# Norms inside the remaining stages, loads in order of use, own banks for a second group, bias parts made once by GpSimd

## What is computed

```python
def _layernorm(x, axis=-1, eps=1e-05):
    m = jnp.mean(x, axis=axis, keepdims=True)
    v = jnp.var(x, axis=axis, keepdims=True)
    return (x - m) / jnp.sqrt(v + eps)
...
x = x + block(_layernorm(x, axis=-1), weights of the block)      # 16 times
```

## Time and profile before

| what | value |
|---|---|
| time, median of 3 runs | 3943.17 us (3942.64 to 3943.90) |
| the profiled execution | 3946.0 us, its span 3944.2 us |
| PE busy | 3227.8 us (82%), 21852 matmuls |
| DVE busy | 2328.7 us (59%) |
| ACT busy | 1703.2 us (43%) |
| POOL busy | 1110.0 us (28%) |
| DMA, mean | 42 GB/s over the span |
| chain that ended last | it ends in the last stage, no line has over 1% of the span |

### The profile page before, as it was taken

The page is one execution under the profiler, slowest core; times in us unless marked ns, Lnnn a source line. Parts: engine busy times, 40 slices in busy tenths (PEclk is TensorE's granted clock), DMA queues, the critical chain, the costliest instruction groups (busy, mean ns, idle before and its releaser), DMA issues. The chain is left out here.

```text
span 3944.2 us, 61118 instructions
## 1 busy us (share of the span) xinstructions
PE 3227.8 (82%) x21852; PEld 1684.0 (43%) x21852; DVE 2328.7 (59%) x5913; ACT 1703.2 (43%) x3496; POOL 1110.0 (28%) x601
## 2 busy tenths in 40 slices
PE   5898899896777777989688895788789786787778
PEld 2444444444666666434233341233234333353336
DVE  4666535445666666465289403898851349945992
ACT  2444433413222222243476425776643445633562
POOL 0000000001111111000289204999940006730771
PEclk8999999895555555999899997999999898998999
DMA  3332221120000000022100000000000101140114
GB/s 131 96 90 80 72 98 53 49 72 34 0 0 0 0 0 0 10 79 70 62 1 0 0 0 0 0 1 1 0 0 0 78 1 43 75 181 1 64 75 171
DMA packets 75647, 166.60 MB, mean 42 GB/s; under 512 B 9440, under 2 KB 46304, under 8 KB 66912
## 3 DMA queue, kind: packets, MB, share of 16 engines
q1 hardware_dynamic: 75488, 164.64, 12.3%
HBM read 120.57 MB, written 44.04 MB: 42 GB/s over the span
## 5 line engine op out<-in xcount | busy, mean ns | idle before, releaser
L1171 PE MATMUL psum<-h_ring,h_parts 128*128 128x4 bf16 (+2 forms) x12288 | 438.1, 170 | 164.4 <-ACT h_ring L1225 157.5
L2007 DVE TENSOR_TENSOR_SCAN s_hh<-psum,s_dbu 128x512 f32<-128x512 f32 x384 | 445.4, 1204 | 154.8 <-POOL s_dbu L1916 100.7
L1171 PEld LDWEIGHTS psum<-h_ring,h_parts 128*128 128x128 bf16 x12288 | 381.6, 105 | 223.3 <-ACT h_ring L1225 193.6
L1916 POOL TENSOR_TENSOR s_dbu<-s_du,s_bb 128x1024 f32<-128x1024 f32 x192 | 448.6, 2353 | 56.8 <-ACT s_bb L1859 53.3
L1225 ACT ACTIVATE h_ring<-h_pre 128x16 f32<-128x16 f32 x1024 | 174.9, 212 | 489.9 <-DVE h_pre L1282 484.3
L1746 PE MATMUL psum<-s_term,w_c 128*128 128x512 f32 x768 | 381.0, 612 | 0.0
L1874 ACT ACTIVATE psum<-s_delta,s_decay 128x512 f32<-128x512 f32 x384 | 263.3, 690 | 147.4 <-DVE s_hh L2007 140.5
L1282 DVE TENSOR_REDUCE h_pre<-psum 128x16 f32<-128x48 f32 x1024 | 170.4, 203 | 133.8 <-PE psum L1171 123.8
L851 DVE TENSOR_TENSOR f_hid<-f_gate,psum 128x512 f32<-128x512 f32 x184 | 126.1, 686 | 202.2 <-PE psum L777 194.6
L838 ACT ACTIVATE f_gate<-psum 128x512 f32<-128x512 f32 x184 | 109.7, 597 | 285.3 <-PE psum L773 285.3
L1524 PE MATMUL psum<-d_h,w_l2f 128*128 128x512 f32 x512 | 221.0, 592 | 0.0
(11 more groups left out here) (432 smaller groups left out, 6447.4 us busy)
## 6 DMA issues: line engine op xcount, KB each, us to landing
...
```

Source lines behind the costliest of these rows:

```text
L1171: mm = nc.tensor.matmul(columns_of(s // BLOCK, grp)[:, s % BLOCK, 0:3 - part, cols], parts[:, part, GROUP * grp + p, :], upper[:, (s - 1) ...
L1916: nc.gpsimd.tensor_tensor(dbu[:, s % 4], du[:, t % 2], both(bb[:, s % 4, :]), ALU.mult).then_inc(dbu_ready, 1)
L2007: nc.vector.tensor_tensor_scan(hh[:, s % 4, half, :], DECAYS[i % 3], dbu[:, s % 4, half, :], 0.0, ALU.mult, ALU.add).then_inc(scan_done, 1)
```

## The change

1. `layernorm` is removed; all 16 stages use `InnerNorm`. It gets `first` and `last` chunks, pieces that can be called one by one, and optionally a semaphore for each chunk's arrival. Each stage gives it banks and scratch tiles of its own.
2. The opening loads in the order of use: the columns of `c32` that the norm needs, chunk 0 of x, the first part of `l0a`, its rest, chunks 1 to 3, the small part of `cbf`, the rest of `c32`, `l2a`, `l3a`. SP waits for the first only. GpSimd casts the small table, now 512 columns. `pick_b` and `pick_c` become a tensor of their own, which the first scan loads into two tiles that are free at its start and GpSimd casts.
3. Latent attention: the norm of chunk 0, the QKV projection, and the other chunks' norm between the steps of turn 0. Turn 1 uses banks 0 and 1 (`low`, `high`). The scores of turn 0 use four banks. The output bias is added before the maxima of turn 0, not behind them. The loop's first two steps wait for `v_kept` and `q1_kept` of turn 1.
4. Recurrent heads: tanh of the weights first, the norms interleaved, the squares of the second one on DVE.
5. Unit attention: chunk 0 is normed before the first projections, chunks 1 to 3 between the second and the third. GpSimd makes the three bf16 parts of phi_b once, into `bias_parts`, for both soft expert stages, which drop their own.

```diff
-def layernorm(g):
...
+    def tensor(self, pe, first=0, last=CHUNKS):
+        for c in range(first, last):
+            if c == first:
+                self.centre_chunk(pe, c)
+            if c + 1 < last:
+                self.centre_chunk(pe, c + 1)
+            self.mean_chunk(pe, c)
...
@@ latent attention, PE @@
+                norm.tensor(pe, 0, 1)
+                pe.wait_ge(g.loaded["l0a_first"], 16)
+                pe.wait_ge(norm.normed, 1)
+                project_qkv(0, 0)
+                norm.centre_chunk(pe, 1)
+                norm.centre_chunk(pe, 2)
                 pe.wait_ge(g.loaded["l0a"], 16)
+                latents(0, 0)
+                norm.mean_chunk(pe, 1)
+                norm.centre_chunk(pe, 3)
+                latents(1, 0)
+                norm.mean_chunk(pe, 2)
+                norm.mean_chunk(pe, 3)
+                queries(0)
+                value_latents(0)
+                latents(0, 1)
+                values(0)
+                latents(1, 1)
...
@@ latent attention, DVE @@
+                norm.vector(dve, 0)
                 dve.wait_ge(g.loaded["l0a"], 16)
+                rope(0, 0)
+                norm.vector(dve, 1)
+                rope(1, 0)
+                norm.vector(dve, 2)
+                left(0, 0)
+                norm.vector(dve, 3)
+                third(0, 0)
...
@@ recurrent heads, ACT @@
                 act.wait_ge(g.loaded["l1a"], 16)
                 nc.scalar.activation(at[:, :], w["a"], ACT.Tanh).then_inc(weights_bounded, 1)
+                norm.scalar(act, 0, 3)
+                invert(0)
+                norm.scalar(act, 3, 4)
+                for j in range(1, CHUNKS):
+                    invert(j)
+                nc.scalar.preload_act_table_set("exp_and_others")
...
@@ selective scan, PE, GpSimd, SP @@
+                norm.tensor(pe)
                 pe.wait_ge(g.loaded[pack], 16)
+                pe.wait_ge(norm.normed, 1)
...
+                pe.wait_ge(norm.normed, CHUNKS)
+                pe.wait_ge(tables_cast, 2)
                 for s in range(3):
                     pick_b(s)
...
+                if tables:
+                    for table, there, loaded in picks:
+                        pool.wait_ge(loaded, 16)
+                        nc.gpsimd.tensor_copy(table.rearrange("p n m -> p (n m)"), wide(there)).then_inc(tables_cast, 1)
...
+                        sp.dma_start(wide(there), g.pick_tables[k]).then_inc(loaded, 16)
...
@@ unit attention, PE (in project) and GpSimd @@
+                    elif m == 2:
+                        norm.tensor(pe, 1, CHUNKS)
+                        pe.wait_ge(norm.logged, CHUNKS)
...
+                pool.wait_ge(g.loaded["l3f"], 16)
+                whole, part = g.w["l3f"]["phi_b"], g.bias_parts
+                nc.gpsimd.tensor_copy(part[:, :], whole).then_inc(hi_kept, 1)
+                pool.wait_ge(hi_kept, 1)
+                nc.gpsimd.tensor_tensor(left[:, :], whole, part[:, :], ALU.subtract).then_inc(rest, 1)
...
@@ soft experts, PE and DVE @@
+                    inner.tensor(pe)
                     for q in range(CHUNKS):
+                        pe.wait_ge(inner.normed, q + 1)
...
-                    pe.wait_ge(bias_set, PARTS)
...
-                    for c in range(PARTS):
-                        at = slice(c * CHUNK, (c + 1) * CHUNK)
-                        nc.vector.tensor_copy(bias[:, at], w["phi_b"][:, at]).then_inc(hi_kept, 1)
...
+                    for c in range(CHUNKS):
+                        inner.vector(dve, c)
...
@@ opening @@
+                    sp.dma_start(tensors["c32"][:, 0:few], args["c32"][:, 0:few]).then_inc(norms_loaded, 16)
+                    sp.dma_start(fixed(g.resid, 0), fixed(args["x"], 0)).then_inc(g.x_loaded[0], 16)
+                    sp.dma_start(tensors["l0a"][:, 0:some], args["l0a"][:, 0:some]).then_inc(g.loaded["l0a_first"], 16)
+                    sp.dma_start(tensors["l0a"][:, some:], args["l0a"][:, some:]).then_inc(g.loaded["l0a"], 16)
+                    for c in range(1, CHUNKS):
+                        sp.dma_start(fixed(g.resid, c), fixed(args["x"], c)).then_inc(g.x_loaded[c], 16)
+                    sp.dma_start(g.wide, args["cbf"]).then_inc(g.table_loaded, 16)
+                    sp.dma_start(tensors["c32"][:, few:], args["c32"][:, few:]).then_inc(g.loaded["c32"], 16)
...
+                    sp.wait_ge(norms_loaded, 16)
```

351 lines of the change are left out of this document (195 added, 156 removed).

## The result

The changed kernel takes 3882.8 us (median of 4 runs, 3876.1 to 3884.9); the kernel before, run beside it, takes 3943.5 us (3942.6 to 3946.9). The ratio is 0.9842, with a 95% interval of 0.9824 to 0.9859: 60.7 us less, where 55.8 were forecast (3887.4). In the profiled executions the span fell from 3944.2 to 3881.3 us, 62.9 less.

The account below looks back on a forecast made before the run. Sixteen stages run one after another on one core, so shorter ways from entry to long loop count: 18.8 + 6.7 + 3.6 + 4.6 + 0 + 10.0 + 12.1 = 55.8 off 3943.2 gives 3887.4 us, range 3873 to 3905.

Parts of the forecast that it names:

- The opening and the latent attention: From span start to the latent attention's loop: reordered loads, interleaved norm and more banks start it at 64.2, not 83.0: -18.8 us.
- PE at 6.2: Opening: PE's first matmul starts at 6.2 us, 11.7 us earlier, after SP's 11 issues and the barrier.
- the term of 0.45 us an issue: Opening: SP's 11 transfers are issued 0.45 us apart, so the last is out at 5.6 us.
- The recurrent heads: Entry to loop: ACT waits 3.4 us for weights, but cuts lie under the norm and the second norm follows chunk by chunk: -6.7 us.
- The scans: Two selective scans, entry to first convolution: the norm inside makes it 13.6 and 11.0 us, a gain of 3.6 and 4.6.
- If the clock holds: Scans' first convolutions: with PE idling only about 3.3 us, staying warm would gain 1.9 and 2.3 us more; left out of the forecast.
- The unit attention: Entry to sums of squares: little gain in the first stretch, sums perhaps at the low clock; taken as 0, bounds -3 and +4.
- little to gain: Unit attention's first stretch: with ACT's norms ahead of its exponentials, DVE's last lift ends 25.6 us after entry against 26.5.
- The soft expert stages: Entry to first logits in both stages: without DVE's bias parts they start at about 14.6 and 17.0 us: -10.0 and -12.1.
- (b): Rival: the norm inside is no shorter than outside where ACT is the chain; 3918.7 us, chance 0.09 with half-way cases.
- (c): Rival: slower, through one more low-clock stretch per scan turn and soft expert tile, 103 us in all; 3991 us, chance 0.02.
- (a): Rival: more overlap, with warm convolutions (-4.2), less waiting in the opening (-4), warm soft-stage transposes (-4); 3875 us, chance 0.10.

Follow-up runs that it names:

- the kernel with everything together: Changed kernel plus late opening issues, scan fillers, unit attention's norm ahead with fillers, two squares before tanh, two turning banks in soft stages: 3866.8 us, ratio 0.9800.

## Why the prediction was right, and where it was not

**The sum.** The time came out 4.6 us from the forecast, but the ways did not come out that near. The seven ways to the loops were forecast at 55.8 us and measured at 66.2, and all seven were too small, by 0.2 to 3.6 us each. What brought the total back was not in the sum: the loops behind the ways took 4.2 us in all (the unit attention alone 5.0), and the medians differ by 2.2 us less than the two profiled executions. The mechanism, a shorter way to each loop, is borne out in all seven stages; that the total is so close is in part luck.

**The opening and the latent attention, -18.8 forecast, -22.4 measured.** PE at 6.2 was wrong (7.91): the term of 0.45 us an issue holds for the first four, but three chunk issues took 0.86 each and the last four 0.5 to 0.6. First chunk normed: 13.2 said, 14.8 measured; end of the first group's last cut 35.1 and 36.3; second pair of the second group 37.1 and 38.1. First scores 49.1 and 48.1: I followed PE's chain, and the row names the stacked query parts, but only 0.33 us behind PE's own work; in the runs with all of x first, with the norm whole and with the late issues PE's own work is last. From the scores to the loop I counted 15.1 us (its terms add up to 14.8) and it took 12.5: the added bias (1.67) lies in front of the maxima as said, but these take 6.45 instead of 7.8. Four banks for two bring 3.3 us (9.8 against 6.45, in the kernel before and in the run with shared banks alike), and I had 2.0. That is the term mis-sized. Another 0.8 is the clock: the turning of the maxima took 1.04 us, and 1.87 in the kernel before, from which I had the 5.3 behind the last maximum. The stall of a_qr went as said in the changed kernel (in four of the variants the addition falls beside the last cast again and takes 0.87 to 1.82 us). It is not shown what the 4.4 us between PE's first matmul and the last cut are made of, beyond that stall (1.1): no run puts the separate norm back there.

**The recurrent heads, -6.7 and -8.2.** The added wait was at its place (tanh 3.5 us after the entry, 3.4 said), the last scaling ended 24.1 after it (24.2 said, from 915.6 - 891.4). Behind that it took 2.0 us instead of 3.4 to the loop: GpSimd's first laying, ahead of PE, 1.0 instead of 2.2, and the projection 1.0 instead of 1.2. That is the difference. The cuts were long done: before, two of them, with both inputs in SBUF, lay beside GpSimd's laying, whose first two steps took 0.69 and 1.37 us where each takes 0.41 now.

**The scans, -3.6 and -4.6 against -4.8 and -4.8.** My norm of 12.4 us at the low clock was too long for the first one: four centre passes took 3.16 instead of 3.75, and the last product ended 11.4 after the entry. "If the clock holds" came true in neither scan of the changed kernel, and in the first scan of four other runs.

**The unit attention, 0 and +3.3.** It is inside my bounds of -3 and +4, but not by my sum. The way to the sums is 1.7 us shorter, and the eight cold passes cost that 1.7 again (I allowed 2.9). The 3.3 are PE at the low clock behind them, 1.6 in each of the first two turns, which I had put at nothing. The scaling beside GpSimd was missed by 0.7 us where I gave it 0 to 1; where the variants hit it, it cost the rest of one GpSimd instruction, as I had taken from the rule. On the first stretch, "little to gain" because ACT has the norms ahead of its exponentials was wrong as a reason: the run with the norm ahead shows 7.8 us of gain there. ACT had been idle 6.4 us for PE's second centre pass, which I had not put in ACT's chain, since I took PE's small groups for the cost of the clock only.

**The soft expert stages, -10.0 and -12.1 against -11.1 and -13.2 (whole stages -10.4 and -16.4).** A round of transposes, copy and hand-over took 1.4 us instead of the 1.8 that I counted, because the transposes ran at the high clock (0.63 instead of 1.11 us); three rounds make the 1.1. The norm outside again and the bias on DVE show that both parts count: the norm is worth 4.5 and 6.6 us on the way to the logits, the bias 9.4 and 8.7 (together more than the 11.1 and 13.2 that both gave, since each hides a part of the other). The extra 3.2 us in the second stage's loop I had not foreseen: from its first logits on, the granted clock of the next 40 us was 0.87, against 0.82 before and 0.82 with the norm outside again, and from the first logits to the end it took 310.9 us, against 314.2 and 315.0. But the kernel with everything together has 0.87 too and 312.8 us, and in the first soft stage 0.80 stands beside 305.2 us and 0.83, with the bias on DVE, beside 308.7. The clock of these 40 us does not by itself give the length, and the cause stays open.

**The rivals.** (b) fell by the run with the norm outside. (c) asked for 27 or more low stretches; what came were a few, in the unit attention. (a), more overlap than counted, was right in its sign: the measured time lies between it and the forecast. Of its three terms the convolutions gave nothing, the opening 3.6 of 4 and the transposes some 2 of 4.
The row at 873.50 again shows the next ACT instruction 1.30 us after the load's start. The rule of the Trainium skill on table loads (ScalarE: Activation LUTs, What ACT_TABLE_LOAD costs: 1.38 us of draining on top) would have given 3879, by the total as near to the measured 3882.8 as the forecast; the rows decide, and they show no draining. That the time came 4.6 us under the forecast has its causes in the ways above.
